# Fourteen normalisation scales moved from GpSimd to ScalarE and VectorE in a one-core hybrid layer, with new instruction orders

## What is computed

```python
x = x + attention(layernorm(x))     # q = n Wq^T, (q n^T) n, no softmax
x = x + ffn(layernorm(x))           # only expert 0 counts; ends in its own layernorm
x = x + rwkv(layernorm(x))          # time mix, then channel mix
x = x + ffn(layernorm(x))

# ffn(y): z = y + relu(y W1 + b1) W2 + b2;  (z - mean) * rsqrt(var + 1e-5) * gamma + beta
# rwkv(x): xa = ln(x; ln1); k, v, r from token-shifted mixes of xa
#          x = x + (sigmoid(r) * wkv(k, v)) Wo^T
#          xc = ln(x; ln2); k2, r2 from token-shifted mixes of xc
#          x + sigmoid(r2 Wr^T) * (square(relu(k2 Wk^T)) Wv^T)
```

## Time and profile before

| | before |
|---|---|
| median of 3 runs | 259.4 us |
| profiled execution, its time | 259.21 us |
| its span, first to last instruction | 257.4 us |
| outside the span | 1.8 us |
| mean granted TensorE clock | 0.997 |
| TensorE busy | 249.5 us |
| ScalarE busy | 231.9 us |
| VectorE busy | 231.2 us |
| GpSimd busy | 133.2 us |

### The profile page before, as it was taken

How to read it: one execution, slowest core, us unless ns; L and a number is a source line. 1 busy time by engine, 2 the same in 40 slices (tenths; PEclk the granted TensorE clock), 3 DMA queues, 4 the chain that set the end, 5 groups by cost and what they waited for, 6 DMA issues and landing times.

```text
span 257.4 us, 5284 instructions
## 1 busy us (share of the span) xinstructions
PE 249.5 (97%) x1504; PEld 187.8 (73%) x1504; DVE 231.2 (90%) x757; ACT 231.9 (90%) x477; POOL 133.2 (52%) x258
## 2 busy tenths in 40 slices
PE   7899999999999999999999999999999999999991
PEld 7687778768767777668759767757848849778771
DVE  5897999999999999999999999999999995955454
ACT  3789789999999999999999999999999999895741
POOL 1656585944961974044596646636604525340640
PEclk9999999999999999999999999999999999999998
DMA  7932224013022240020763422205204424374297
GB/s 196 308 99 45 42 42 84 0 28 56 3 40 43 41 84 1 0 45 0 134 105 52 74 48 45 42 0 98 67 0 85 81 56 70 55 144 87 45 187 179
DMA packets 17772, 18.10 MB, mean 70 GB/s; under 512 B 1488, under 2 KB 11600, under 8 KB 17744
## 3 DMA queue, kind: packets, MB, share of 16 engines
q0 software_dynamic: 6480, 11.80, 27.0%
q1 hardware_dynamic: 10848, 5.84, 8.1%
q10 hardware_dynamic: 416, 0.14, 0.2%
HBM read 3.87 MB, written 2.10 MB: 23 GB/s over the span
## 4 chain that ended last, share of the span: by engine, by line
PE 94%; DVE 2%; DMA 1%; ACT 1%; POOL 1%; issue 0%; DVEq 0%; POOLq 0%; ACTq 0%
PE bank L1155 21%; PE bank L1164 21%; PE bank L1232 11%; PE bank L1226 11%; PE bank L1114 7%; PE bank L1213 3%; PE bank L1243 3%; PE bank L1197 3%; PE bank L1207 3%; PE bank L1202 3%; PE bank L1142 3%; PE bank L1127 2%; PE bank L1275 1%; DMA R<-in_hidden 1%; PE bank L1175 1%; PE bank L1135 1%
## 5 line engine op out<-in xcount | busy, mean ns | idle before, releaser
L1164 PEld LDWEIGHTS bank<-W,f_h 128*128 128x128 f32 x480 | 58.2, 192 | 8.7 <-issue 8.6
L1155 PE MATMUL bank<-f_yT,W 128*128 128x512 f32 x128 | 61.2, 593 | 0.0
L1164 PE MATMUL bank<-W,f_h 128*128 128x128 f32 x480 | 60.2, 275 | 0.0
L1155 PEld LDWEIGHTS bank<-f_yT,W 128*128 128x128 f32 x128 | 21.9, 190 | 16.3 <-issue 11.3
L1232 PEld LDWEIGHTS bank<-FWv,KK 128*128 128x128 f32 x256 | 30.6, 192 | 3.4 <-issue 2.3
L1226 PE MATMUL bank<-XK,FWk 128*128 128x512 f32 x64 | 32.0, 597 | 0.0
L1232 PE MATMUL bank<-FWv,KK 128*128 128x128 f32 x256 | 31.8, 275 | 0.0
L828 ACT ACTIVATE f_y<-R,f_yn_nb,f_yn_rs 128x128 f32<-128x128 f32 x64 | 26.3, 490 | 0.9 <-POOL f_yn_nb L350 0.9
L895 ACT ACTIVATE f_h<-bank,B 128x512 f32<-128x512 f32 x32 | 21.2, 681 | 5.5 <-PE bank L1155 4.2
L390 POOL DMA_DIRECT2D R<-G x7 | 6.3, 897 | 36.4 <-DVE G L686 36.4
L895 ACT ACTIVATE f_h<-bank,B1C 128x512 f32<-128x512 f32 x32 | 21.4, 682 | 0.1
(11 more groups left out here) (159 smaller groups left out, 620.3 us busy)
## 6 DMA issues: line engine op xcount, KB each, us to landing
R<-BETA POOLq DMA_DIRECT2D x16, 256.0 KB, 3.6
R<-f_zg POOLq DMA_DIRECT2D x14, 256.0 KB, 4.0
R<-N POOLq DMA_DIRECT2D x8, 256.0 KB, 3.4
R<-in_hidden SPq DMA_DIRECT2D x7, 256.0 KB, 5.0
R<-G POOLq DMA_DIRECT2D x7, 256.0 KB, 3.4
out_x<-R SPq DMA_DIRECT2D x7, 256.0 KB, 2.3
W<-in_w SPq DMA_DIRECT2D x2, 256.0 KB, 4.5
BETA<-in_beta SPq DMA_DIRECT2D x1, 256.0 KB, 4.6
```

Of the source, the lines that this page charges most:

```text
L1155: t_.matmul(banks[bank][:], W1[:, n * P:(n + 1) * P], at(f.yT, b)[:], start=True, stop=True).then_inc(f.h_psum[n], 1)
L1164: last = t_.matmul(banks[bank][:, j * C:(j + 1) * C], at(f.h, b)[:, n, j * P:(j + 1) * P], W2[:, n, :], start=False, stop=(n == H - 1), sk ...
```

## The change

Fourteen of the normalisations lose `shift`, `power` and `bias` on GpSimd. They are all eight of channel mix (`ncm`), batches 1 to 3 of attention (`na`), and batches 0 to 2 of the first feed-forward (`f1.norm`). In their place ScalarE runs `norm_log` and the existing `z_root`, and VectorE runs `norm_bias`. Four attention scales, thirteen of the feed-forwards and all of time mix stay on GpSimd.

```diff
@@ VectorE
+            def norm_bias(b, n):
+
+                dve.wait_ge(*n.scale.done(b, "rs"))
+                v.scalar_tensor_tensor(n.nb[b % 2][:], n.mv[b % 2][:, :, 0], -1.0, n.rs[b % 2][:], ALU.mult, ALU.mult).then_inc(n.scale.sem(b), 1)
@@ ScalarE
+            def norm_log(b, n):
+                act.wait_ge(const_ready, 8)
+                act.wait_ge(n.mv_ready, b + 1)
+                if b >= 2:
+                    act.wait_ge(*n.ready.done(b - 2, "all"))
+                a.activation(n.ve[b % 2][:], n.mv[b % 2][:, :, 1], ACT.Ln, bias=K_EPS[:, 0:1]).then_inc(n.scale.sem(b), 1)
```

The four lists of GpSimd, VectorE, ScalarE and TensorE are all written anew (SyncE's is not touched). The starts of them, where the prediction walks through them:

```diff
@@ GpSimd, the first calls
-            shift(1, na); power(1, na); bias(1, na); shift(2, na); power(2, na); bias(2, na); shift(3, na)
-            power(3, na); shift(0, f1.norm); bias(3, na); power(0, f1.norm); bias(0, f1.norm); shift(1, f1.norm)
-            power(1, f1.norm); bias(1, f1.norm); shift(4, na); shift(5, na); power(4, na); ffn_residual(0, f1)
+            shift(4, na); power(4, na); ffn_residual(0, f1); shift(5, na); bias(4, na); ffn_residual(1, f1)
+            shift_twice(0); power(0, nt); bias(0, nt); power(5, na); shift(3, f1.norm); bias(5, na)
@@ VectorE
-            first_normed(1); attn_stats(1); mean_var(1, na); attn_stats(2); mean_var(2, na); attn_stats(3)
-            attn_out(0, 1); mean_var(3, na); bias_diagonal(); ffn_stats(0, f1); mean_var(0, f1.norm)
+            first_normed(1); attn_stats(1); mean_var(1, na); attn_stats(2); bias_diagonal(); mean_var(2, na)
+            norm_bias(1, na); attn_stats(3); norm_bias(2, na); attn_out(0, 1); ffn_stats(0, f1); mean_var(3, na)
+            mean_var(0, f1.norm); attn_stats(4); norm_bias(3, na); norm_bias(0, f1.norm); attn_out(1, 0)
@@ ScalarE
-            first_log(0); first_root(0); first_log(1); first_root(1); gram_evacuate(0, 1); attn_evacuate(0, 0)
-            proj_evacuate(0, 1); attn_normed(1); attn_normed(2); gram_evacuate(1, 2); attn_evacuate(1, 0)
-            attn_evacuate(2, 1); proj_evacuate(1, 2); attn_normed(3); gram_evacuate(2, 3); ffn_normed(0, f1)
-            proj_evacuate(2, 3); ffn_evacuate(0, f1, 2); attn_evacuate(3, 1); ffn_normed(1, f1); relu(0, f1, 0, 2)
+            first_log(0); first_root(0); first_log(1); first_root(1); norm_log(1, na); gram_evacuate(0, 1)
+            z_root(1, na); attn_evacuate(0, 0); norm_log(2, na); proj_evacuate(0, 1); z_root(2, na); attn_normed(1)
+            attn_normed(2); gram_evacuate(1, 2); norm_log(3, na); norm_log(0, f1.norm); z_root(3, na)
+            attn_evacuate(1, 0); proj_evacuate(1, 2); z_root(0, f1.norm); attn_normed(3); gram_evacuate(2, 3)
+            ffn_normed(0, f1); attn_evacuate(2, 2); proj_evacuate(2, 3); norm_log(1, f1.norm); ffn_evacuate(0, f1, 0)
...
+            relu(1, f1, 2, 4); relu(1, f1, 1, 0); z_root(2, f1.norm); relu(1, f1, 3, 5); ffn_normed(2, f1)
+            tmix_normed(0); decay_rates(); tmix_evacuate(0, 5); ffn_evacuate(2, f1, 0); attn_evacuate(4, 4)
@@ TensorE
             attn_transpose(0, 0); attn_gram(0, 1); attn_proj(0, 1); attn_apply(0, 1); attn_transpose(1, 0)
-            attn_gram(1, 2); attn_transpose(2, 1, x1.ready(0)); attn_proj(1, 2); attn_gram(2, 3); bias_rows()
-            attn_apply(1, 2); attn_transpose(3, 1); attn_proj(2, 3); attn_gram(3, 4)
-            ffn_transpose(0, f1, 2, x1.ready(1)); attn_apply(2, 3); hidden_up(0, f1, 0, 2)
+            attn_gram(1, 2); attn_proj(1, 2); bias_rows(); attn_gram(2, 3); attn_transpose(2, 2, (proj_ready, 2))
+            attn_apply(1, 0); attn_transpose(3, 1); attn_proj(2, 3); attn_gram(3, 4)
+            ffn_transpose(0, f1, 0, x1.ready(1)); attn_apply(2, 3); hidden_up(0, f1, 2, 0)
```

Towards the end, the work that TensorE does behind the last `cmix_down(7, 3)` changes too:

```diff
-            hidden_up(5, f2, 2, 7, (f2.h_ready[1], 6)); ffn_transpose(6, f2, 5); cmix_down(7, 3, 1)
-            ffn_down(5, f2, 0, 0); ffn_down(5, f2, 1, 0); ffn_down(5, f2, 2, 0); ffn_down(5, f2, 3, 0)
+            cmix_down(7, 0, 4); cmix_down(7, 1, 4); hidden_up(5, f2, 2, 1); ffn_down(5, f2, 0, 5); cmix_down(7, 2, 4)
+            ffn_down(5, f2, 1, 5); cmix_down(7, 3, 4); ffn_transpose(6, f2, 1, (f2.h_ready[2], 6))
+            ffn_down(5, f2, 2, 5); ffn_down(5, f2, 3, 5); hidden_up(6, f2, 0, 1)
```

More of the change, by code:

```diff
@@ L1297, in _ @@
-            attn_gram(5, 6, (m2_ready, 1)); hidden_up(3, f1, 1, 0, (xnT_ready, 6)); ffn_down(3, f1, 0, 5)
-            hidden_up(3, f1, 3, 6, (gram_ready, 6)); hidden_up(3, f1, 2, 0, (f1.h_ready[1], 4)); product_k(1, 3)
-            attn_transpose(6, 4, (f1.zg_ready, 3)); attn_proj(5, 6, (f1.h_ready[3], 4)); ffn_down(3, f1, 1, 5)
-            attn_gram(6, 1, gate.done(0, "rl")); attn_apply(5, 6); product_o(0, 0)
-            ffn_transpose(4, f1, 3, expo.done(1, "diff")); product_v(1, 1, (gram_ready, 7))
@@ new lines, in _ @@
+            attn_apply(1, 0); attn_transpose(3, 1); attn_proj(2, 3); attn_gram(3, 4)
+            ffn_transpose(0, f1, 0, x1.ready(1)); attn_apply(2, 3); hidden_up(0, f1, 2, 0)
+            hidden_up(0, f1, 0, 1, (xnT_ready, 4)); hidden_up(0, f1, 1, 7, b2_rows.done(0, "column"))
+            hidden_up(0, f1, 3, 5); ffn_transpose(1, f1, 3, x1.ready(2)); ffn_down(0, f1, 0, 2); ffn_down(0, f1, 1, 2)
+            ffn_down(0, f1, 2, 2); ffn_down(0, f1, 3, 2); attn_proj(3, 4); hidden_up(1, f1, 0, 5)
@@ new lines, in _ @@
+            attn_gram(6, 1, (f1.h_ready[1], 4)); product_k(1, 2, (f1.zg_ready, 3))
+            attn_apply(5, 3, (f1.h_ready[3], 4)); attn_proj(6, 1); attn_transpose(6, 0, (b1_ready, 1))
+            product_v(1, 5); ffn_down(3, f1, 1, 7); ffn_down(3, f1, 2, 7); ffn_down(3, f1, 3, 7)
+            ffn_transpose(4, f1, 0, (xnT_ready, 7)); attn_apply(6, 2, expo.done(1, "diff")); product_o(0, 1)
+            hidden_up(4, f1, 0, 0); hidden_up(4, f1, 1, 2, x1.ready(6)); hidden_up(4, f1, 3, 3)
+            product_r(1, 0, (f1.h_ready[0], 5)); hidden_up(4, f1, 2, 5, (ev_ready, 2))
@@ new lines, in _ @@
+            cmix_transpose(0, 1); product_r(2, 0, (f1.h_ready[1], 6)); ffn_transpose(6, f1, 4, expo.done(2, "diff"))
+            product_o(1, 1, (xc_ready, 1)); attn_apply(7, 6); hidden_up(6, f1, 0, 4); product_v(2, 7)
+            ffn_down(5, f1, 1, 5); cmix_up(0, 0, 1); ffn_down(5, f1, 2, 5); tmix_transpose(3, 6, x1.ready(7))
+            ffn_down(5, f1, 3, 5); gate_product(0, 3); cmix_up(0, 3, 6, (xa_ready, 4))
+            cmix_up(0, 1, 4, (f1.h_ready[0], 7)); cmix_down(0, 0, 1)
+            hidden_up(6, f1, 2, 6, square[3].done(0, "relu")); cmix_up(0, 2, 4, square[1].done(0, "relu"))
@@ new lines, in _ @@
+            cmix_transpose(1, 7, (m2_ready, 3)); hidden_up(6, f1, 3, 2); cmix_down(0, 1, 1)
+            ffn_start(6, f1, 4, square[2].done(0, "relu")); hidden_up(6, f1, 1, 7, (xc_ready, 2)); product_k(3, 6)
+            cmix_down(0, 2, 1); ffn_down(6, f1, 0, 4); cmix_down(0, 3, 1); cmix_up(1, 0, 2, (f1.h_ready[3], 7))
+            cmix_up(1, 2, 3); product_v(3, 7); product_o(2, 0); cmix_up(1, 1, 2, square[0].done(1, "relu"))
+            gate_product(1, 6); ffn_transpose(7, f1, 3, square[2].done(1, "relu"))
@@ new lines, in _ @@
+            tmix_transpose(6, 0, square[3].done(3, "relu")); cmix_down(3, 1, 7); ffn_down(1, f2, 1, 2)
+            gate_product(3, 6, (f2.h_ready[2], 2)); cmix_transpose(4, 4); ffn_down(1, f2, 2, 2); cmix_down(3, 2, 7)
+            cmix_down(3, 3, 7); ffn_down(1, f2, 3, 2); ffn_transpose(2, f2, 3); product_k(6, 4); cmix_up(4, 2, 0)
+            hidden_up(2, f2, 2, 1, gate.done(5, "rl")); hidden_up(2, f2, 0, 3)
+            product_o(5, 0, square[2].done(4, "relu")); cmix_up(4, 3, 6, cgate.done(3, "rl"))
@@ new lines, in _ @@
+            cmix_down(5, 1, 3); gate_product(5, 5, (u1_ready, 7)); ffn_down(3, f2, 0, 7)
+            hidden_up(3, f2, 2, 0, (f2.h_ready[1], 4)); cmix_down(5, 2, 3); ffn_down(3, f2, 1, 7)
+            product_r(7, 6, (ev_ready, 8)); cmix_transpose(6, 2, (f2.zg_ready, 2)); ffn_down(3, f2, 2, 7)
+            ffn_down(3, f2, 3, 7); cmix_down(5, 3, 3); ffn_transpose(4, f2, 2); cmix_up(6, 0, 0); cmix_up(6, 2, 1)
+            cmix_up(6, 1, 2, (f2.yT_ready, 5)); hidden_up(4, f2, 0, 0, square[0].done(6, "relu"))
```

439 lines of the change are left out of this document (206 added, 233 removed).

## The result

The changed kernel takes **260.56 us** (median of 5 runs, 260.50 to 260.88); the kernel before took 259.4 us beside it (5 runs, 258.55 to 259.99). The ratio is 1.0051, 95% interval 1.0029 to 1.0073: half a per cent slower. The profiled execution took 260.62 us, its span is 258.8 us (257.4 before).

The account below looks back on a forecast made before the run. TensorE was taken as the bound, with ScalarE and VectorE nearly full between 60 and 220 us. 0.9 us (head) + 0.3 (middle) = 1.2 us on the profiled 259.21 gave 260.4 us; 8-in-10 range 258.2 to 263.0.

Parts of the forecast that it names:

- the head: Start of the kernel: extra logs and roots in ScalarE's queue and a delay at time mix of batch 0, 0.9 us slower.
- the first place: ScalarE's queue ahead of the first `hidden_up`: two logs and two roots more start it at about 18.85, 0.7 us later.
- The other 0.2: Time mix of batch 0: its transposes start at about 34.7, 0.9 us later than before, adding another 0.2 us.
- The hop: Last channel-mix batch, `mean_var` start to first normalised row: 1.2 us instead of 2.2, 1.0 us earlier; no gain booked.
- The price of a pair: ScalarE's queue: a log takes 0.19 us, or 0.33 with the root right behind; a root 0.11; 0.30 to 0.44 a pair.
- VectorE: nothing booked: VectorE gains 14 `norm_bias`, 1.6 us, covered by 3.9 us without work between 60 and 220 and 5.4 afterwards.
- I book 0.3 us for the wait that remains: Full stretch and its end: ScalarE's eight pairs, mostly covered by idle time, cost 0.3 us, between 0 and 2.4.
- The ends keep their steps: The 5.9 us ahead of TensorE's work and the 5.4 us behind it keep their steps.
- The third: ScalarE becomes the bound of the full stretch, all eight pairs and eight biases are waited for: 263.4 us, chance 0.12.
- its term of 2.4: Full stretch and its end: TensorE waits for each of ScalarE's eight pairs, 2.4 us.
- The first: Channel mix from batch 3 and the rest after 18 us: shorter hops fill TensorE's gaps, 257.7 us, chance 0.2.
- The fourth: GpSimd lets go of VectorE: 14 powers taken away speed VectorE by at most 0.4 us, 260.0 us, chance 0.02.

Follow-up runs that it names:

- Experiment 1: Kernel before with five spare log and root pairs in ScalarE's list, where the changed kernel has its first five; nobody waits for them: 259.94 us.
- experiment 9: Changed kernel, channel-mix scales except batch 4 back on GpSimd, `bias(6, f1.norm)` and `bias(3, nt)` ahead of the channel-mix shifts: 260.80 us.
- experiment 4: Kernel before with sixteen spare log and root pairs on ScalarE, two ahead of each `cmix_normed`; nobody waits for them: 262.05 us.
- experiment 5: Kernel before with sixteen spare `norm_bias` on VectorE, two behind each `mean_var` of channel mix; nobody waits for them: 260.41 us.
- 11: Changed kernel with six scales of the second feed-forward normalisation (f1 3 to 7, f2 1) on GpSimd instead of ScalarE: 260.61 us.
- experiment 12: Kernel before with `ffn_residual(7, f2)` issued ahead of `ffn_sum(4)` in GpSimd's list: 259.61 us.
- 6: Kernel before with seven scales of the second feed-forward normalisation (f1 3 to 7, f2 0 and 1) moved from ScalarE to GpSimd: 260.20 us.
- experiment 7: Kernel before, eight channel-mix scales moved to ScalarE and VectorE, six second feed-forward scales (f1 3, 5, 6, 7, f2 0, 1) to GpSimd: 261.79 us.

## Why the prediction was right, and which of its steps was not

The number was right: 260.4 us forecast, 260.56 measured, and slower by more than 0.3% was the likeliest side. It was right by luck in its parts: the sum had 0.9 us for the head, 0.3 for the middle and nothing behind, and measured were 0.6, 1.5 and -0.7. TensorE's end came 2.1 us later instead of 1.2, and the two errors cancelled.

- **The head** held in its mechanism. `hidden_up` was forecast at 18.85 and came at 18.77; `attn_normed(1)` at 9.2 to 9.3 and came at 9.09; the transposes of N of batch 0 at 34.7 and came at 34.48. Experiment 1 shows the mechanism, pairs in ScalarE's queue, by itself, with 0.35 to 0.6 us. The mean over executions is 0.64 us (17.98 to 18.62), for the 0.7 of the first place. The other 0.2, for time mix of batch 0, did not come: its transposes were 0.65 us later (33.83 to 34.48), no more than `hidden_up`.
- **The hop** held: 1.29 us measured, 1.2 forecast. It was seen to be worth something at batch 7 only, within the new lists (experiment 9).
- **The price of a pair** held as a place in the queue: 0.33 when adjacent (218.17 to 218.50), 0.19 and 0.10 else. What it costs the kernel is 0.19 us a pair in the full stretch of the old lists (experiment 4). The Trainium skill, "ScalarE: Activation LUTs", section "Rules for kernel authors", would have had 0.6 us a pair (an estimate from its 0.3 us per ACTIVATE); the run has a third of that, so taking the row was right.
- **"VectorE: nothing booked"** failed. 0.075 us each (experiment 5), 1.05 us for 14: VectorE's 3.9 us without work were no cover. That they don't lie where the instruction stands is my reading; in the new lists seven `norm_bias` are part of the 0.36 us below.
- **"I book 0.3 us for the wait that remains"** failed as a size: the stretch lost 1.5 us, where I had 0.2 + 0.3. And it failed as a reason. I asked what the moved instructions cost in the new lists, and that is 0.36 us up to 216 us (experiment 9), less than the shorter hop of batch 7 gives back there. I walked through the new lists in the head and at time mix of batch 0, and no further. One place later, at time mix of batch 1, two unmoved steps had changed places, and that is 0.85 of the 1.5 us. It is read from the trace and stays in experiments 9 and 11; a kernel with `bias(1, nt)` ahead of `back_shift(1)` again wasn't tried. Of the other 0.65 us (0.36 more between 77 and 97 us, 0.48 between 157 and 177, less elsewhere), 0.36 go with the moved scales of channel mix, and the rest is not traced to a cause. The longest waits left are 0.34 us at 167.56, for VectorE's XK, and 0.31 us at 146.36, for VectorE's G; why VectorE is late there is open.
- **The ends keep their steps** failed: 0.7 us less behind TensorE. The steps are the same, but the last sum lands earlier against VectorE's end, and the store of batch 6 is out of the way of the last two (experiment 12).
- **Rivals.** The third, ScalarE as the bound, had part of the right mechanism for the wrong kernel: with the old lists moving channel mix alone costs 2.3 us. That this is near its term of 2.4 is chance: some 0.7 of it follow waits of `norm_bias`, and a spare pair costs 0.19 and not 0.30. The new lists bring the whole of it, six scales more in the head included, to 1.2 us. The first, shorter hops, is real at one batch of eight. The fourth, GpSimd letting go of VectorE, is not seen: 14 powers less, and VectorE's instructions start no closer together (below). But the prediction's row was thin: of the eight products of line 650 only one ran while a power that had started before it was still running (at 167.56, 0.664 us). The product of two SBUF tiles at line 631 did so three times, with 1.217 to 1.219 us, against 1.196 to 1.221 in the other five; that bears the reading out.

## What to carry to other kernels

When TensorE is the bound and two engines beside it are nearly full, the price is one-sided: a small instruction put into a full queue costs most of its place in the queue (0.19 us of 0.29 for a pair, 0.075 us for a bias), and one taken out gained nothing (experiments 6 and 11), presumably because TensorE had no wait there to give back; where it had waits, in experiment 7, a pair gave 0.1 us. In these queues written out by hand, what stands between the steps of a chain cost more than which engine runs them: two calls in the wrong place cost 10 us here, and by the trace, an exchange of unmoved steps cost 0.85 us, more than the moved scales of channel mix in the same lists. So when a change comes with new orders, walk every chain that feeds the bound through the new lists, the untouched ones first.
